# Latents projected inside attention, and attention's loop over batches written out

## The chip, the cores and the metric

The kernel runs on one core of a Trainium2 chip. The metric is the device time of one execution in microseconds, as the median of several runs. The engines of the core work in parallel and meet at semaphores only: TensorE (PE in the profile, with its weight loads as PEld), VectorE (DVE), ScalarE (ACT), GpSimd (POOL), and SyncE (SP), which here issues nearly all DMAs.

## The reference

Everything is float32. `x` is [8, 1024, 256]: 8 batches of 1024 tokens.

```python
x = layernorm(x + attention(x))
x = layernorm(x + expert_choice_moe(x))   # 8 experts, hidden 1024; untouched by the change

def attention(x):                         # 16 heads of 64, causal
    latent = x @ w_kv_down                # [.., 256] @ [256, 128]
    kv = latent @ w_kv_up                 # [.., 128] @ [128, 2048]
    k, v = kv[..., :1024], kv[..., 1024:]
    q = x @ w_q                           # [.., 256] @ [256, 1024]
    att = softmax(mask(q @ k.T * 64 ** -0.5))
    return (att @ v) @ w_out
```

## The kernel before

**Stages.** `latent_stage`, `attention_stage`, `output_stage`, `choose_stage` and `expert_stage` run one after the other, each a block of its own that begins once every engine has left the one ahead. Only the first two are touched.

**latent_stage** (from line 37). For each batch, 4 float32 matmuls of 128x512 (two halves of the tokens, two halves of the 256 channels) form the latents in a PSUM tile `a_ps`. ScalarE copies them out (line 94) and stores them to a DRAM tensor `lat_d` (line 96). A loop runs twice over four batches.

**attention_stage** (from line 101). The unit of work is a pair of heads: 8 batches with 8 pairs each, `n` = 0 to 63, `m = n % 8`. A pair has 16 slots `s`, one for each of 8 query tiles and 2 heads. Every engine walks through the slots with its own written order (`slots`), which interleaves three pairs. In slot `s` TensorE does the following:

- the scores of slot `s + 3` (lines 373, 374: the queries split into a high and a low float32r part, against the keys), once ScalarE has finished the exponentials of two slots earlier (`exp_done`);
- the transposes of the probabilities of slot `s` (line 389, `turn`) into `t_ps`, or into `s_ps` in slot 14;
- projections for later pairs into the single bank `j_ps`: queries of pair `n + 2` in slots 12 and 15 (`Q_AT`, lines 421 to 423, six matmuls each), keys of pair `n + 1` in slots 2 and 5 (`K_AT`), values of pair `n + 1` in slots 7 and 9 (`V_AT`, line 444);
- the products with the values, `pv` (line 405), in slots 14, 1 and 4.

VectorE takes the masked maximum of each slot (line 598) and its reciprocal sum (line 603), half of the copies out of `t_ps` (line 662), and the low parts of the queries and keys (lines 611, 614). ScalarE has the exponentials (line 505), the other half of the copies (line 581), the high parts (line 513) and the copies of the values (line 518). GpSimd scales the probabilities (line 247). SyncE stores `y`, loads weights, and places the split queries and keys into `q_hl`, `k_hh` and `k_lz` by DMA, ten issues for each pair.

**Once in a batch, in pair m = 6:** `x_split` makes the parts `b_xt_hi` and `b_xt_lo` of the next batch's x in slots 0, 2, 4 and 6 (lines 534 and 626), and `l_split` the parts `b_lat_hi` and `b_lat_lo` of its latents in slots 14 and 15 (lines 541 and 632). The latents come from `lat_d` by a DMA on SyncE's queue (line 284), which waits until the values of pair 7 are projected.

**The loop.** `over_pairs` (line 184) writes out `first()` and the first half of pair 0, then has a hardware loop of 7 turns on each engine, whose body is 8 whole pairs from the middle of pair 0 to the middle of the next batch's pair 0, and then writes out the last batch. In the loop a wait compares with a register, and instructions that set such registers stand between the others. The loop turns back between slots 7 and 8 of a batch's first pair. `first()` projects the queries, keys and values of pair 0 one after the other through `j_ps`.

Of the kernel before, what the change touches and what calls it, by code (L numbers as in the profile page):

```python
# [36 lines left out]
def latent_stage(nc, x_t, w_down, lat_d):  # L37

    XB = 4
    with ExitStack() as ctx:  # L40
        sb = lambda n, s, d=F32: ctx.enter_context(nc.sbuf_tensor(n, s, d))
        sem = lambda n: ctx.enter_context(nc.semaphore(n))
        wd = sb("wd", [P, KC, RANK])
        xt = [sb(f"a_xt{v}", [P, KC, T]) for v in range(XB)]
        lat = [sb(f"a_lat{u}", [P, T]) for u in range(2)]
        ps = [ctx.enter_context(nc.psum_tensor(f"a_ps{u}", [P, T], F32)) for u in range(2)]
        w_in, lat_done, lat_copied = sem("a_w_in"), sem("a_lat_done"), sem("a_lat_copied")
        x_in = [sem(f"a_x_in{v}") for v in range(XB)]
        lat_out = [sem(f"a_lat_out{u}") for u in range(2)]
        block = ctx.enter_context(nc.Block())  # L50

        @block.sync
        def _(sp):
            def load_x(b, v):
                sp.dma_start(xt[v][:], x_t.rearrange("(k p) (b t) -> p k b t", p=P, t=T)[:, :, bass.ds(b, 1), :]
                             .rearrange("p k o t -> p k (o t)")).then_inc(x_in[v], 16)

            sp.dma_start(wd[:], w_down.rearrange("(k p) r -> p k r", p=P)).then_inc(w_in, 16)
            for v in range(XB):
                load_x(v, v)  # L60
            with sp.Fori(1, B // XB) as i:
                for v in range(XB):
                    b = XB * i + v

                    sp.wait_ge(lat_done, b - XB + 2)
                    load_x(b, v)

        @block.tensor
        def _(pe):

            for signal in (lat_done, lat_copied, *lat_out):
                pe.sem_inc(signal, 1)
            pe.wait_ge(w_in, 16)
            with pe.Fori(0, B // XB) as i:
                for v in range(XB):
                    b = XB * i + v
                    pe.wait_ge(x_in[v], 16 * i + 16)

                    pe.wait_ge(lat_copied, b if v else b + 1)
                    for c in range(T // HALF):  # L80
                        for k in range(KC):
                            mm = pe.matmul(ps[v % 2][:, c * HALF:(c + 1) * HALF], wd[:, k, :],
                                           xt[v][:, k, c * HALF:(c + 1) * HALF], start=(k == 0), stop=(k == KC - 1))
                    mm.then_inc(lat_done, 1)

        @block.scalar
        def _(act):
            with act.Fori(0, B // XB) as i:
                for v in range(XB):
                    b, u = XB * i + v, v % 2  # L90
                    act.wait_ge(lat_done, b + 2)

                    act.wait_ge(lat_out[u], 16 * (XB // 2 * i + v // 2) + 1)
                    act.activation(lat[u][:], ps[u][:], ACT.Copy).then_inc(lat_copied, 1)
                    act.wait_ge(lat_copied, b + 2)
                    act.dma_start(lat_d[bass.ds(b, 1), :, :].rearrange("o p t -> p (o t)"),
                                  lat[u][:]).then_inc(lat_out[u], 16)
            for u in range(2):
                act.wait_ge(lat_out[u], 16 * (B // 2) + 1)


def attention_stage(nc, x_t, w_q, w_k, w_v, lat_d, y_d):
# [9 lines left out]
    with ExitStack() as ctx:  # L112
# [7 lines left out]
        lat = sb("b_lat", [P, T])  # L120

# [32 lines left out]
        const_ready, x_in, lat_in = sem("const_ready"), sem("b_x_in"), sem("b_lat_in")  # L154
# [31 lines left out]
        def over_pairs(eng, first, slots):  # L186

            first()
            slots(0, 0, 0, 2)
            with eng.Fori(0, B - 1) as b:
                for m in range(NPAIR):
                    slots(NPAIR * b + m, m, 1, 2)
                    slots(NPAIR * b + m + 1, (m + 1) % NPAIR, 0, 2)
            for n in range(NPAIRS - NPAIR, NPAIRS):
                after = min(2, NPAIRS - 1 - n)
                if n % NPAIR:
                    slots(n, n % NPAIR, 0, after)  # L200
                slots(n, n % NPAIR, 1, after)
# [3 lines left out]
        L_SPLIT = [(NPAIR - 2, s) for s in (14, 15)]  # L205
# [65 lines left out]
        def _(sp):  # L271
# [11 lines left out]
            def load_latent(b):  # L283
                sp.dma_start(lat[:], lat_d[bass.ds(b, 1), :, :].rearrange("o p t -> p (o t)")).then_inc(lat_in, 16)
# [79 lines left out]
        def _(pe):  # L364
# [87 lines left out]
            def first():  # L452
                pe.wait_ge(const_ready, 8)
                for c in range(2):
                    project_q(0, 0, c)
# [1183 lines left out]
```

## Time and profile before

| | us |
|---|---|
| median of 3 runs (3380.58 to 3381.19) | 3380.62 |
| the profiled execution | 3380.8 |
| its span in the trace | 3379.1 |
| latent stage and the start of attention, up to the first scores | 81.7 |
| attention, from the first scores to its last store of y | 2121.5 |
| the rest (output, choice, experts) | about 1176 |

The table's stages are read from the times at which TensorE's first scores (81.66) and SyncE's last store of `y` (2203.2) start. The span is counted from the first instruction, and 1.7 us lie around it. Positions in the trace are microseconds from the span's start.

### The profile page before, as it was taken

What the parts mean: (1) busy time and instruction counts of PE and PEld (TensorE: products, weight loads), DVE (VectorE), ACT (ScalarE), POOL (GpSimd) and SP (SyncE); (2) the same over time, 40 slices, a digit from 0 to 9 for tenths busy, and PEclk for the clock granted to TensorE, in tenths of its full rate; (3) what the DMA queues carried; (4) which work ended last, traced back from release to release, by engine and by line L of the source; (5) the groups of instructions that cost most, each with busy time, mean ns of one, the idle gap of its engine ahead of it and who ended that gap; (6) DMA issues with size and microseconds to landing.
All of it is one profiled execution on the core that took longest, in us unless ns stands there. A gap on an engine that the chain in (4) does not pass through costs nothing. (4 is left out here: it accounts for less than half of the span.)

```text
span 3379.1 us, 69338 instructions
## 1 busy us (share of the span) xinstructions
PE 3130.4 (93%) x20382; PEld 2506.5 (74%) x20382; DVE 2092.6 (62%) x5849; ACT 1868.3 (55%) x4063; POOL 1371.8 (41%) x1543
## 2 busy tenths in 40 slices
PE   5999999999999999999999999979908999999995
PEld 2777676777677677777677777679907999899995
DVE  1667666667666666666666666656684555555555
ACT  2667676667666676667666666633203433333335
POOL 0334343334344343334333343312214565645555
PEclk7999999999999999999999999989958999999998
DMA  6444444445445444444445444267502333323327
GB/s 209 99 121 117 101 115 108 108 98 126 99 110 121 108 112 112 114 98 119 112 100 121 114 110 98 66 254 267 186 33 65 68 76 70 76 34 68 76 55 209
DMA packets 184389, 376.22 MB, mean 111 GB/s; under 512 B 23872, under 2 KB 108224, under 8 KB 181952
## 3 DMA queue, kind: packets, MB, share of 16 engines
q1 hardware_dynamic: 153152, 316.91, 35.8%
q0 software_dynamic: 29696, 50.48, 7.5%
q8 instruction: 176, 2.88, 0.4%
q10 hardware_dynamic: 1152, 4.19, 0.3%
q14 instruction: 213, 1.74, 0.2%
HBM read 123.97 MB, written 79.76 MB: 60 GB/s over the span
## 5 line engine op out<-in xcount | busy, mean ns | idle before, releaser
L247 POOL TENSOR_SCALAR prob<-prob,inv 128x128 f32<-128x128 f32 (+7 forms) x1024 | 770.4, 752 | 1301.8 <-DVE inv L603 1301.8
L598 DVE CUSTOM_DVE_ANT_0 s_ps<-s_ps,mask 128x128 f32<-128x128 f32 (+7 forms) x1024 | 781.5, 763 | 664.1 <-PE s_ps L374 649.0
L505 ACT ACTIVATE prob<-s_ps,neg_max 128x128 f32<-128x128 f32 (+7 forms) x1024 | 759.5, 742 | 348.5 <-DVE neg_max L598 327.0
L373 PE MATMUL s_ps<-k_hh,q_hl 128*128 128x512 f32 (+3 forms) x1536 | 591.7, 386 | 46.5 <-ACT prob L505 28.5
L389 PE MATMUL t_ps<-ident,prob 128*128 128x128 f32 x4096 | 611.7, 274 | 1.0 <-ACT prob_t L581 0.5
L405 PE MATMUL o_ps<-prob_t,v 128*64 128x512 f32 (+3 forms) x3072 | 537.5, 492 | 1.5 <-DVE y L620 1.5
L581 ACT ACTIVATE prob_t<-t_ps 128x512 f32<-128x512 f32 (+3 forms) x704 | 376.8, 535 | 290.3 <-PE t_ps L389 284.4
L374 PE MATMUL s_ps<-k_lz,q_hl 128*128 128x512 f32 (+3 forms) x1536 | 516.0, 348 | 0.0
L389 PEld LDWEIGHTS t_ps<-ident,prob 128*128 128x128 f32 x4096 | 478.7, 141 | 47.5 <-DVE prob_t L662 1.2
L373 PEld LDWEIGHTS s_ps<-k_hh,q_hl 128*128 128x128 f32 x1536 | 290.6, 189 | 195.8 <-issue 82.3
L405 PEld LDWEIGHTS o_ps<-prob_t,v 128*64 128x64 f32 x3072 | 204.0, 136 | 285.1 <-issue 266.4
L662 DVE COPY prob_t<-t_ps 128x128 f32<-128x128 f32 (+3 forms) x704 | 321.6, 457 | 29.3 <-PE t_ps L389 29.3
L374 PEld LDWEIGHTS s_ps<-k_lz,q_hl 128*128 128x128 f32 x1536 | 292.4, 190 | 32.6
L1424 PE MATMUL e_y<-w_hi,hid_hi 128*128 128x256 f32 (+1 forms) x1088 | 308.0, 283 | 0.0
L1426 PE MATMUL e_y<-w_hi,hid_lo 128*128 128x256 f32 (+1 forms) x1088 | 303.6, 279 | 0.0
L1425 PE MATMUL e_y<-w_lo,hid_hi 128*128 128x256 f32 (+1 forms) x1088 | 303.5, 279 | 0.0
L1473 ACT ACTIVATE raw<-e_h,b1s 128x512 f32<-128x512 f32 (+3 forms) x320 | 186.4, 601 | 139.4 <-PE e_h L1411 105.4
L1528 DVE CAST hid_hi<-raw 128x512 fp32r<-128x512 f32 (+3 forms) x320 | 173.8, 550 | 120.5 <-ACT raw L1473 110.3
L1462 ACT ACTIVATE yg<-yb,gate 128x256 f32<-128x256 f32 x128 | 59.2, 503 | 333.1 <-DVE yb L1552 308.1
L1349 POOL DMA_INDIRECT acc_d<-yg,idx x128 | 210.6, 1645 | 75.1 <-ACT yg L1462 41.2
L1409 PE MATMUL e_h<-tok_hi,w_hi 128*128 128x512 f32 (+3 forms) x640 | 227.3, 355 | 13.5 <-ACT raw L1473 6.8
L1411 PE MATMUL e_h<-tok_hi,w_lo 128*128 128x512 f32 (+3 forms) x640 | 225.5, 352 | 0.0
(157 smaller groups left out, 5547.5 us busy)
## 6 DMA issues: line engine op xcount, KB each, us to landing
k_hh<-k_high SPq DMA_DIRECT2D x256, 256.0 KB, 4.5
q_hl<-q_high SPq DMA_DIRECT2D x128, 256.0 KB, 3.6
q_hl<-q_low SPq DMA_DIRECT2D x128, 256.0 KB, 4.1
k_lz<-k_low SPq DMA_DIRECT2D x128, 256.0 KB, 4.9
y_d<-y SPq DMA_DIRECT2D x128, 256.0 KB, 4.3
c_yt<-y_d SPq DMA_DIRECT2D x16, 2048.0 KB, 8.3
w_raw<-w SPq DMA_DIRECT2D x16, 1024.0 KB
a_xt<-x_t SPq DMA_DIRECT2D x8, 1024.0 KB, 9.5
```

The source lines that it names most:

```text
L247: pool.tensor_scalar(pr, pr, inv[:, s % 4:s % 4 + 1], 1.0, ALU.mult, ALU.mult).then_inc(norm_done, 1)
L373: pe.matmul(out, q_hl[u][h][:, cols], k_hh[u][h][:, w], start=True, stop=False)
L374: mm = pe.matmul(out, q_hl[u][h][:, cols], k_lz[u][h][:, w], start=False, stop=True)
L389: mm = pe.transpose(turned_in(s, k)[:, j * P:(j + 1) * P], prob[s % 4][:, (first + j) * P:(first + j + 1) * P], ident[:])
L405: mm = pe.matmul(o_ps[64 * h:64 * h + 64, off:HALF], v[u][:, k, 64 * h:64 * h + 64], prob_t[g][:, h, k, off:HALF], start=(k == 0), stop=(k ...
L505: act.activation(prob[s % 4][:, 0:(q + 1) * P], s_ps[s % 2][:, 0:(q + 1) * P], ACT.Exp, scale=-1.0, bias=neg_max[:, s % 4:s % 4 + 1], accu ...
L581: act.activation(prob_t[g][:, h, b0:b0 + count, q % 4 * P:(q % 4 + 1) * P], turned_in(s, k)[:, 0:count * P].rearrange("p (j c) -> p j c", ...
L598: dve.tensor_tensor_reduce(part, part, mask[:, T - (q + 1) * P:T], 1.0, -MASKED, ALU.add, ALU.min, neg_max[:, s % 4:s % 4 + 1]).then_inc(m ...
L662: dve.tensor_copy(prob_t[g][:, h, b0:b0 + count, q % 4 * P:(q % 4 + 1) * P], turned_in(s, k)[:, 0:count * P].rearrange("p (j c) -> p j c", ...
L1424: pe.matmul(out, hid_hi[:, m, cols], W.w2_hi[u][:, w], start=(m == 0), stop=False)
L1425: pe.matmul(out, hid_hi[:, m, cols], W.w2_lo[u][:, w], start=False, stop=False)
L1426: mm = pe.matmul(out, hid_lo[:, m, cols], W.w2_hi[u][:, w], start=False, stop=(m == HC - 1))
```

## The change

`latent_stage` and the DRAM tensor `lat_d` go. `attention_stage` takes `w_down` and keeps it in three tiles: `wd`, `wd_hi`, `wd_lo`. A new function `project_l` forms the latents of one half of a batch with six float32r matmuls (high by high, high by low, low by high, for two channel halves) from the parts of x that the query projection already uses. For batch 0 this stands at the head of `first()`. For the next batch it stands in pair m = 6, in slots 10 and 14 (`L_AT`). ScalarE's `l_split`, one slot later, first copies the latents from PSUM to `lat` and then makes `lat_hi`. The queries of pair `n + 2` in that pair wait for these copies, since they use the same bank. In `first()` the second halves of all projections go to `o_ps` in place of `j_ps` (`bank`). `over_pairs` writes out all 64 pairs on TensorE, ScalarE, VectorE and GpSimd. SyncE keeps its loops, without the load of the latents.

```diff
-def latent_stage(nc, x_t, w_down, lat_d):
...
-            slots(0, 0, 0, 2)
-            with eng.Fori(0, B - 1) as b:
-                for m in range(NPAIR):
-                    slots(NPAIR * b + m, m, 1, 2)
-                    slots(NPAIR * b + m + 1, (m + 1) % NPAIR, 0, 2)
-            for n in range(NPAIRS - NPAIR, NPAIRS):
+            for n in range(NPAIRS):
                 after = min(2, NPAIRS - 1 - n)
-                if n % NPAIR:
-                    slots(n, n % NPAIR, 0, after)
-                slots(n, n % NPAIR, 1, after)
+                for g in range(2):
+                    slots(n, n % NPAIR, g, after)
...
-        L_SPLIT = [(NPAIR - 2, s) for s in (14, 15)]
+        L_AT = (10, 14)
...
+        def latents(n, m, s):
+            return L_AT.index(s) if m == NPAIR - 2 and s in L_AT and not last_batch(n) else None
+        def bank(n, c):
+            return o_ps if c and isinstance(n, int) and n == 0 else j_ps
...
-                if reload and m_is(m, NPAIR - 2):
-                    sp.wait_ge(proj_done, 6 * n + 12)
-                    sp.sem_inc(passed, 1)
-                    load_latent(b + 1)
...
+            def project_l(b, c):
+                first = isinstance(b, int) and b == 0
+                if c == 0:
+                    pe.wait_ge(x_low, 4 * b + 4)
+                if first:
+                    pe.wait_ge(wd_low, 1)
+                elif c == 0:
+                    pe.wait_ge(v_copied, 2 * NPAIR * b)
+                else:
+                    pe.wait_ge(low_done, 4 * NPAIR * b + 1)
+                out = bank(b, c)
+                for k in range(KC):
+                    pe.matmul(out[:], wd_hi[:, k, :], xt_hi[:, k, halves(c)], start=(k == 0), stop=False)
+                    pe.matmul(out[:], wd_hi[:, k, :], xt_lo[:, k, halves(c)], start=False, stop=False)
+                    mm = pe.matmul(out[:], wd_lo[:, k, :], xt_hi[:, k, halves(c)], start=False, stop=(k == KC - 1))
+                mm.then_inc(lat_done, 1)
+            def latents_copied(b, c):
+                pe.wait_ge(l_copied, 2 * b + c + 1)
...
+                elif fresh:
+                    latents_copied(n >> 3, c)
...
                     turn(n, s)
+                    if latents(n, m, s) is not None:
+                        project_l((n >> 3) + 1, latents(n, m, s))
...
             def l_split(b, i):
-                act.wait_ge(lat_in, 16 * b + 16)
+                act.wait_ge(lat_done, 2 * b + i + 1)
                 if not (isinstance(b, int) and b == 0):
-                    act.wait_ge(proj_done, 6 * NPAIR * b - 2)
+                    act.wait_ge(proj_done, 6 * NPAIR * b)
+                act.activation(lat[:, halves(i)], bank(b, i)[:], ACT.Copy).then_inc(l_copied, 1)
+                act.wait_ge(l_copied, 2 * b + i + 1)
                 act.activation(lat_hi[:, halves(i)], lat[:, halves(i)], ACT.Copy).then_inc(l_high, 1)
...
-                    if (m, s) in L_SPLIT and not last_batch(n):
-                        l_split((n >> 3) + 1, L_SPLIT.index((m, s)))
+                    if latents(n, m, s - 1) is not None:
+                        l_split((n >> 3) + 1, latents(n, m, s - 1))
```

TensorE at the start of attention, before: six matmuls of the first query half, all halves in `j_ps`.

```order
L421 MATMUL j_ps<-b_xt_hi,wqk_hi 128x512 [waits b_x_low,b_w_low,const_ready]
L422 MATMUL j_ps<-b_xt_lo,wqk_hi 128x512
L423 MATMUL j_ps<-b_xt_hi,wqk_lo 128x512
L421 MATMUL j_ps<-b_xt_hi,wqk_hi 128x512
L422 MATMUL j_ps<-b_xt_lo,wqk_hi 128x512
L423 MATMUL j_ps<-b_xt_hi,wqk_lo 128x512
L421 MATMUL j_ps<-b_xt_hi,wqk_hi 128x512 [waits low_done]
```

The same place now (the first half of the latents, then the head of the second, which has a bank of its own).

```order
L358 MATMUL j_ps<-b_xt_hi,wd_hi 128x512 [waits b_wd_low,b_x_low,const_ready]
L359 MATMUL j_ps<-b_xt_lo,wd_hi 128x512
L360 MATMUL j_ps<-b_xt_hi,wd_lo 128x512
L358 MATMUL j_ps<-b_xt_hi,wd_hi 128x512
L359 MATMUL j_ps<-b_xt_lo,wd_hi 128x512
L360 MATMUL j_ps<-b_xt_hi,wd_lo 128x512
L358 MATMUL o_ps<-b_xt_hi,wd_hi 128x512 [waits b_wd_low]
```

The latents stand ahead of the queries, and a second half no longer waits for VectorE to empty the bank.

TensorE in pair m = 6, slot 10 and the head of slot 11, now (line 323 is the transposes, 307 and 308 the scores).

```order
L323 MATMUL t_ps<-ident,prob 128x128 [waits copied_d]
L323 MATMUL t_ps<-ident,prob 128x128
L358 MATMUL j_ps<-b_xt_hi,wd_hi 128x512 [waits v_copied,b_x_low]
L359 MATMUL j_ps<-b_xt_lo,wd_hi 128x512
L360 MATMUL j_ps<-b_xt_hi,wd_lo 128x512
L358 MATMUL j_ps<-b_xt_hi,wd_hi 128x512
L359 MATMUL j_ps<-b_xt_lo,wd_hi 128x512
L360 MATMUL j_ps<-b_xt_hi,wd_lo 128x512
L307 MATMUL s_ps<-k_hh,q_hl 128x512 [waits exp_done]
```

Before, the scores followed the transposes directly; six matmuls stand between them, and the first waits for the copy of the values. The second six stand in the same way in slot 14, ahead of `pv`.

VectorE in pair m = 6, slots 11 and 12, before (line 598 is the maximum, 662 the copy of the transposed tiles).

```order
L598 ISA s_ps,neg_max<-s_ps,mask 128x1024 [waits scores_done]
L598 ISA neg_max 128x1
L603 RECIPROCAL inv<-total 128x1 [waits exp_done]
L660 REGISTER_ALU
L662 COPY prob_t<-t_ps 128x2x128 [waits pv_done1,turned]
L594 REGISTER_ALU
L598 ISA s_ps,neg_max<-s_ps,mask 128x1024 [waits scores_done]
```

And now (line 574 is the maximum, 640 the copy).

```order
L574 ISA s_ps,neg_max<-s_ps,mask 128x1024 [waits scores_done]
L574 ISA neg_max 128x1
L579 RECIPROCAL inv<-total 128x1 [waits exp_done]
L640 COPY prob_t<-t_ps 128x2x128 [waits pv_done1,turned]
L608 TENSOR_TENSOR b_lat_lo<-b_lat,b_lat_hi 128x512 [waits b_l_high]
L574 ISA s_ps,neg_max<-s_ps,mask 128x1024 [waits scores_done]
```

The low part of the latents, which stood in slot 14, is now ahead of the maximum of the last slot's scores and waits there for ScalarE; the register instructions are gone.

## Rows read from the trace of the kernel before

**Rows 1.** The page's head: busy time, share of the span and instructions of each engine.

```profile
PE 3130.4 (93%) x20382; PEld 2506.5 (74%) x20382; DVE 2092.6 (62%) x5849; ACT 1868.3 (55%) x4063; POOL 1371.8 (41%) x1543
```

**Rows 2.** Busy time of each engine in the middle of attention, with granted clock.

```profile
170.00:2230.00 2060.00, 1993.90 (x12437) 1462.94 (x12436) 1361.20 (x4092) 1376.67 (x3170) 797.15 (x1043) 0.99 0.46 111
```

**Rows 3.** TensorE's waits from 170 to 2200: total us, times, longest.

```profile
PE s_ps L373 <- ACT prob L505: 25.9, 69, 2.5
PE s_ps L373 <- issue: 12.9, 4, 3.4
PE j_ps L444 <- DVE k_low L614: 3.9, 7, 0.6
```

**Rows 4.** The same windows view, from slot 12 to the next pair's slot 12.

```profile
1795.85:1828.38 32.53, 32.22 (x202) 23.67 (x202) 21.62 (x67) 22.01 (x52) 12.91 (x18) 1.00 0.45 106
1860.87:1894.02 33.15, 32.28 (x202) 23.68 (x202) 24.01 (x71) 23.87 (x56) 13.89 (x18) 1.00 0.45 105
2024.61:2057.22 32.61, 32.27 (x202) 23.66 (x202) 21.63 (x67) 22.06 (x52) 12.90 (x18) 1.00 0.45 105
```

**Rows 5.** The same view of the six pairs in which the loop turns back, and their sum.

```profile
335.88:371.79 35.91, 32.48 (x202) 23.77 (x203) 21.64 (x67) 22.06 (x52) 12.89 (x18) 1.00 0.48 116
600.08:637.75 37.67, 34.06 (x202) 25.16 (x203) 21.69 (x67) 22.07 (x52) 12.89 (x18) 0.95 0.45 110
...
sum 220.91, PE 201.25 PEld 148.33 DVE 129.99 ACT 132.56 POOL 77.37; mean PE 33.54 PEld 24.72 DVE 21.66 ACT 22.09 POOL 12.89
```

**Rows 6.** Timeline of the start: start us, us, engine, line, instruction, idle before.

```profile
1.37 22.07 SPq L55 DMA_DIRECT2D a_xt<-x_t  x8
...
6.69 16.34 PE L82 MATMUL a_ps<-a_xt,wd 128*128 128x512 f32 x32 [6.69 <-DMA a_xt<-x_t]
...
47.78 0.37 SPq L281 DMA_DIRECT2D b_xt<-x_t  x1
...
50.32 3.62 POOL L239 MEMSET k_lz<- 128x1024 f32 x4
...
54.36 2.17 ACT L534 ACTIVATE b_xt_hi<-b_xt 128x512 fp32r<-128x512 f32 x4
...
55.01 2.99 DVE L626 TENSOR_TENSOR b_xt_lo<-b_xt,b_xt_hi 128x512 fp32r<-128x512 f32 x4 [55.01 <-ACT b_xt_hi L534]
...
58.70 0.63 PE L422 MATMUL j_ps<-b_xt_lo,wqk_hi 128*128 128x512 f32 x1
...
59.13 0.63 PE L423 MATMUL j_ps<-b_xt_hi,wqk_lo 128*128 128x512 f32 x1
...
66.88 0.47 PE L430 MATMUL j_ps<-b_lat_hi,wqk_hi 128*128 128x512 f32 x1 [1.50 <-DVE q_low L611]
...
81.66 0.44 PE L373 MATMUL s_ps<-k_hh,q_hl 128*128 128x128 f32 x1 [4.63 <-DMA k_lz<-k_low]
```

**Rows 7.** Timeline, TensorE, first turn of the loop: start, us, instruction, idle before.

```profile
364.66 0.49 PE L373 MATMUL s_ps<-k_hh,q_hl 128*128 128x512 f32 x1 [3.13 <-issue]
```

**Rows 8.** Timeline of pair m = 6 of a late batch, slots 10 to 14.

```profile
1891.63 0.59 ACT L518 ACTIVATE v<-j_ps 128x512 f32<-128x512 f32 x1
...
1891.89 0.47 PE L373 MATMUL s_ps<-k_hh,q_hl 128*128 128x512 f32 x1
...
1894.02 0.50 PE L373 MATMUL s_ps<-k_hh,q_hl 128*128 128x512 f32 x1 [0.31 <-ACT prob L505]
...
1895.73 0.48 PE L421 MATMUL j_ps<-b_xt_hi,wqk_hi 128*128 128x512 f32 x1
...
1897.21 0.22 PE L373 MATMUL s_ps<-k_hh,q_hl 128*128 128x128 f32 x1
...
1899.25 0.69 DVE L611 SCALAR_TENSOR_TENSOR q_low<-j_ps,q_high 128x512 fp32r<-128x512 f32 x1 [0.33 <-ACT q_high L513]
1899.33 2.37 PE L405 MATMUL o_ps<-prob_t,v 128*64 128x512 f32 x16
```

**Rows 9.** DMA of instructions in the written-out last batch, 1959 to 2189 (packets, MB).

```profile
q8 instruction: 11, 0.18, 0.3%
```

More of the change, by code:

```diff
@@ L34 @@
 BH = B * NE
-def latent_stage(nc, x_t, w_down, lat_d):
[L39 to L99, printed above, removed]
@@ L102, in attention_stage @@
[L102 removed]
+def attention_stage(nc, x_t, w_down, w_q, w_k, w_v, y_d):
     NPAIRS = B * NPAIR
@@ L415, in project_q @@
                     pe.wait_ge(x_low, 4 * (n >> 3) + 4)
-                    if not (isinstance(n, int) and n == 0):
-                        pe.wait_ge(v_copied, 2 * n)
+                if first:
+                    latents_copied(0, c)
+                elif fresh:
+                    latents_copied(n >> 3, c)
+                elif c == 0:
+                    pe.wait_ge(v_copied, 2 * n)
                 else:
                     pe.wait_ge(low_done, 4 * n + 1)
+                out = bank(n, c)
                 for k in range(KC):
-                    pe.matmul(j_ps[:], wqk_hi[u][:, k, :], xt_hi[:, k, halves(c)], start=(k == 0), stop=False)
-                    pe.matmul(j_ps[:], wqk_hi[u][:, k, :], xt_lo[:, k, halves(c)], start=False, stop=False)
-                    mm = pe.matmul(j_ps[:], wqk_lo[u][:, k, :], xt_hi[:, k, halves(c)], start=False, stop=(k == KC - 1))
+                    pe.matmul(out[:], wqk_hi[u][:, k, :], xt_hi[:, k, halves(c)], start=(k == 0), stop=False)
+                    pe.matmul(out[:], wqk_hi[u][:, k, :], xt_lo[:, k, halves(c)], start=False, stop=False)
+                    mm = pe.matmul(out[:], wqk_lo[u][:, k, :], xt_hi[:, k, halves(c)], start=False, stop=(k == KC - 1))
                 mm.then_inc(proj_done, 1)
@@ L428, in project_k @@
                     pe.wait_ge(l_low, 2 * (n >> 3) + 2)
-                pe.wait_ge(low_done, 4 * n + 2 + c)
-                pe.matmul(j_ps[:], wqk_hi[u][:, KC, :], lat_hi[:, halves(c)], start=True, stop=False)
-                pe.matmul(j_ps[:], wqk_hi[u][:, KC, :], lat_lo[:, halves(c)], start=False, stop=False)
-                pe.matmul(j_ps[:], wqk_lo[u][:, KC, :], lat_hi[:, halves(c)], start=False, stop=True
+                pe.wait_ge(low_done, 4 * n + (1 if isinstance(n, int) and n == 0 else 2) + c)
+                out = bank(n, c)
+                pe.matmul(out[:], wqk_hi[u][:, KC, :], lat_hi[:, halves(c)], start=True, stop=False)
+                pe.matmul(out[:], wqk_hi[u][:, KC, :], lat_lo[:, halves(c)], start=False, stop=False)
+                pe.matmul(out[:], wqk_lo[u][:, KC, :], lat_hi[:, halves(c)], start=False, stop=True
                           ).then_inc(proj_done, 1)
             def project_v(n, u, c):
+                first = isinstance(n, int) and n == 0
                 if c == 0:
                     pe.wait_ge(w_in[u], 48 * (n >> 1) + 48)
-                    pe.wait_ge(lat_in, 16 * (n >> 3) + 16)
+                    pe.wait_ge(l_copied, 2 * (n >> 3) + 2)
+                if first:
+                    pe.wait_ge(low_done, 3 + c)
+                elif c == 0:
                     pe.wait_ge(low_done, 4 * n + 4)
@@ L453, in first @@
                 pe.wait_ge(const_ready, 8)
+                for c in range(2):
+                    project_l(0, c)
                 for c in range(2):
@@ L666, in slots @@
                         x_split((n >> 3) + 1, X_SPLIT.index((m, s)))
-                    if (m, s) in L_SPLIT and not last_batch(n):
-                        l_split((n >> 3) + 1, L_SPLIT.index((m, s)))
+                    if latents(n, m, s - 1) is not None:
+                        l_split((n >> 3) + 1, latents(n, m, s - 1))
                     if s - 1 in Q_AT and after >= 2:
```

36 lines of the change are left out of this document (21 added, 15 removed).

## The prediction

> **What bounds the kernel now.** I read the page's head first: TensorE is busy for 93% of the span [rows 1], so the question is which TensorE time the change removes or adds, and not which engine is relieved. The windows view of attention says the same of the long middle part: 1993.9 us of 2060 busy at a granted clock of 0.99, with VectorE and ScalarE at two thirds [rows 2]. Next come TensorE's waits in that stretch [rows 3]. There are only three that count: a short one on ScalarE's exponentials in every pair, 12.9 us put down to "issue", that is, to nothing that the profile shows, in 4 places, and 0.6 us once in a batch on the low part of a key. To see what a pair costs I cut attention at slot 12. An ordinary pair takes 32.53 us, the pair m = 6 with the splits takes 33.15, a pair of the written-out last batch 32.61 [rows 4]. The six pairs in which the loop turns back take 220.91 us together [rows 5]. The reader should see three things in these rows: attention is a chain of TensorE work with hardly a gap, so every matmul added to it lengthens it by its own duration; the turns of the loop are the one large gap; and the last batch is already the new form of the code, with its price per pair. The start is a separate matter: up to 81.66 us there is no score [rows 6].
>
> **1. The start.** The latent stage runs from 0.9 to 47.8 us, where attention's first DMA is issued; from there the first scores are 33.9 us away [rows 6]. Now x is loaded for attention at once. Its issue should stand where the first load of x stands, at 1.37. The first x of the latent stage was used 5.3 us after its issue (6.69), attention's x by 6.6 us after it (47.78 to 54.36). I take 5.6, so 7.0. From the first high part to the last low part it is 3.64 us (54.36 to 58.00): 10.7. The twelve matmuls of the latents start there on a cold array, 0.43 us apart (58.70 to 59.13): 5.1 us, so 15.8. The twelve query matmuls cost 5.1 us if still cold, and 12 x 0.245 = 2.9 if the clock has come up by then, as it did during the latent stage's first stretch: 18.7 to 20.9. ScalarE's and VectorE's pieces (0.6 and 0.7 us) no longer stand between the halves, since these have two banks, and the copies of the latents pass beside the query matmuls. The first key matmul then follows, and from it to the first scores it was 14.8 us before (66.88 to 81.66), most of it DMA of queries and keys in a row on SyncE's queue. Sum: 33.5 to 35.7, and perhaps 1 less for the keys' second bank. I take 34.0, so **-47.7 us**, with -45 and -50 as ends. Cover that is gone: GpSimd's fills, which ended 6.2 us after the issue of x (47.78 to 53.94), end before x is split, as they did [rows 6]. The weights' load is issued right behind x and is wanted only after the latents.
>
> **2. The turns of the loop.** The six pairs are 220.91 - 6 x 32.53 = 25.7 us longer than ordinary ones [rows 5]. The gap itself is some 3.1 us, with every engine at its own branch at that time, TensorE's put down to "issue" [rows 7]. The second of the pairs shown has a granted clock of 0.95 over its length, and the six hold 201.25 us of busy TensorE against 6 x 32.23 in ordinary ones, 7.9 us more: after such a gap part of the work runs at the lower of the two clocks. The seventh turn, which leaves the loop, costs nothing. In the changed kernel TensorE's first backward branch stands in the output stage, and no engine but SyncE has one in attention: **-25.7 us**. SyncE's own branch falls between its keys and its next weights, where no one waits. The Trainium skill, "Runtime: NRT & Kernel Launch", section "Instruction fetch mechanics", says that a taken branch to a place outside the fetched window has to wait for a DMA of that code. The gap of 3.13 us agrees.
>
> **3. Code without registers.** The last batch is written out already: 32.61 us for each of its pairs against 32.53 [rows 4], without any loop gap. The 0.08 to 0.09 us appear ahead of the values' projection. What causes them I can't tell from the trace. Over 56 pairs that were in the loop: **+5.0 us**, with 0 and +10 as ends. By the same section of the Trainium skill, code is fetched block by block ahead of its use, and the crossing is mostly hidden. If it were wholly free the sum would be 5 us lower; the row of the last batch decides for the 5.
>
> **4. The latents' matmuls.** In the pair m = 6 of batches 0 to 6, twice six matmuls. Six such matmuls of the query projection take 1895.73 to 1897.21, 1.48 us [rows 8]. 14 x 1.48 = **+20.7 us**. Nothing hides them, since TensorE has no idle time there. The latents' matmuls of the old stage don't count again; they went with it.
>
> **5. The waits that come with them.** I follow the pair of rows 8 with the new order, on its own times.
> - Slot 10: TensorE has its transposes done at 1891.89, but the bank is free only when the values' copy ends at 1892.22: 0.4 us of wait.
> - Slot 12: the wait of 0.31 us for an exponential (1894.02) is gone, since TensorE comes 1.9 us later: -0.3.
> - Slots 11 to 13: ScalarE now has two copies of 0.6 us (latents, high part) instead of none, and VectorE the low part (0.7 us) between the maxima of slots 14 and 15. This maximum and the copy of transposed tiles behind it come about 2.5 us later, TensorE about 1.9 later. The transposes of slots 12 and 13 and the scores that need the last exponential then wait 0.2 + 0.5 + 0.35 = about 1.0 us.
> - Slot 14: the second six want the bank from VectorE's low part of the queries. That ended at 1899.94, when TensorE had reached `pv` at 1899.33; the lag stays nearly the same after both slid: 0.6 us less what was already waited, so 0.3.
> - Slot 15: `pv` (2.3 us) stands between the latents and the queries that wait for their copy, so nothing there. The keys of pair 8 come in slot 2 of pair 7, far behind the split.
>
> This adds up to +1.1 to +1.4 us; I take **1.15 x 7 = +8.0 us**. The ends: -0.3 x 7 = -2 if VectorE and ScalarE keep up, and +3 us a batch, +21, if every one of these waits is passed on in full. SyncE loses a wait and a load of 0.5 MB there, which costs and gives nothing. The 0.6 us that pair 6 already waits for a key's low part [rows 3] stays.
>
> **Sum** on the profiled execution, 3380.8 us: -47.7 - 25.7 + 5.0 + 20.7 + 8.0 = -39.7, which gives 3341.1. The profile is within 0.2 us of the median, so I predict 3341 for the median as well.
>
> **The rivals.**
> - *The latents' chain costs more.* In pair 6 VectorE and ScalarE are already the fullest of the batch, 24.0 and 23.9 us of 33.15 [rows 4], and one more wait of a microsecond or two would be passed from the maximum to the exponential to the scores. At +3 us a batch the time is 3341 + 13 = 3354. For it: three engines wait for one another within four slots. Against it: the same pair took the four splits of x at a price of 0.6 us in all.
> - *The latents' waits vanish.* If TensorE's added 3 us of work give the others enough room, step 5 is -2 and the time 3331. For it: the others have 8 us spare in the pair. Against it: the low part stands in front of a maximum in the written order.
> - *The branch time isn't won.* If the six gaps were fetching that has to be done at some point of a batch anyway, writing the code out would spread them: 3367. Against it: the written-out last batch, with 11 packets of instructions on that queue [rows 9], has no gap of this kind in its pairs.
> - *Slower than before: fetching straight code holds TensorE up.* It would stand anywhere in the 56 pairs. Without step 3 the sum is 3336.1; slower by 0.2% begins at 3387.6, so this needs 51.5 / 56 = 0.92 us for each pair, about one gap like that of rows 7 in every third pair. A gap in every pair would give 3336 + 56 x 3.1 = 3510. It decides once fetching for TensorE takes longer than executing. The last batch shows a tenth of the 0.92, so I give it little. The Trainium skill's section named above speaks against it as well.
> - *The change doesn't do what it says.* The order of instructions shows that it does; I leave no chance to this.
>
> **How the numbers follow.** My forecast (3334 to 3348): 0.66. Latents' chain dearer, about 3354: 0.14. Waits vanish, about 3331: 0.11. Branch time not won, 3367, or half of it: 0.05. Slower, 3388 and beyond: 0.02. Something between, 3374 to 3387: 0.02. The range takes in both chain cases, with the ends of the start (3 us either way) and of step 3 (5 us either way) partly on top: 3327 to 3358. It leaves out the last three cases and the far ends of the two before, some 0.15 in all. A measurement of this kernel can tell about 0.2% (7 us) from no change. Faster by more than that: 0.96; within it: 0.02; slower: 0.02.
>
> **What would show it.** In the profile of the changed kernel: the first scores of attention at 32 to 36 us; no row with "issue" of 3 us ahead of a score in slot 8, and a granted clock of 1.00 in all pairs; ordinary pairs of 32.6 us through all batches; the pair m = 6 at 37 us (33.15 + 2.96 + 0.09 + 1.15) and waits on ScalarE, VectorE and the values' copy in slots 10 to 14; TensorE's matmuls from `wd` 84 in number after the first twelve, about 1.5 us for each six. I'm wrong if ordinary pairs take more than 33 us, if pair 6 takes more than 40, or if the first scores start after 40 us.

## The result and the profile after

The changed kernel takes 3335.3 us (median of 4 runs, 3334.5 to 3335.9) against 3380.6 for the kernel before beside it: a ratio of 0.9869, with a 95% interval of 0.9857 to 0.9881. The profiled execution took 3334.5 us, with a span of 3332.8. The forecast was 3341 (3327 to 3358), so the sign, the size and most of the terms held. On the later occasions the kernel before had medians of 3377 to 3384 us, so an absolute time from one occasion can be compared with one from another only to some 4 us. In the traces a stage can be cut out, but each is of one execution: the first scores came at 33.42 us here and at 32.61 in the changed kernel's second trace, and the first pair behind them took 25.36 and 26.84 us, at a granted clock of 0.93 and 0.84.

The start in the trace after (start, us, engine, line, instruction, idle before):

```profile
1.36 0.45 SPq L223 DMA_DIRECT2D b_xt<-x_t  x1
...
6.54 2.19 ACT L505 ACTIVATE b_xt_hi<-b_xt 128x512 fp32r<-128x512 f32 x4 [3.03 <-DMA b_xt<-x_t]
7.20 2.50 DVE L602 TENSOR_TENSOR b_xt_lo<-b_xt,b_xt_hi 128x512 fp32r<-128x512 f32 x4 [3.24 <-ACT b_xt_hi L505]
...
9.80 0.76 PE L358 MATMUL j_ps<-b_xt_hi,wd_hi 128*128 128x512 f32 x1 [9.80 <-DVE b_xt_lo L602]
...
15.06 0.51 PE L382 MATMUL j_ps<-b_xt_hi,wqk_hi 128*128 128x512 f32 x1
...
18.33 0.47 PE L392 MATMUL j_ps<-b_lat_hi,wqk_hi 128*128 128x512 f32 x1 [0.26 <-DVE q_low L587]
...
33.42 0.44 PE L307 MATMUL s_ps<-k_hh,q_hl 128*128 128x128 f32 x1 [10.40 <-DMA k_lz<-k_low]
```

These answer to [rows 6]. The first scores come at 33.42 us where they came at 81.66, 48.2 us earlier. TensorE's last wait there is on the DMA of the keys.

TensorE's waits in attention after, from 50 to 2150, in full down to 1 us in total: us, times, longest (the answer to [rows 3]):

```profile
PE s_ps L307 <- ACT prob L476: 19.8, 67, 0.7
PE j_ps L410 <- DVE k_low L590: 4.5, 7, 0.7
PE j_ps L358 <- DVE q_low L587: 2.6, 7, 0.4
PE j_ps L358 <- ACT v L489: 1.1, 7, 0.2
```

The row with "issue" is gone. Two new rows stand in its place, seven waits each, both on the latents' bank: 0.16 us for the copy of the values in slot 10 and 0.36 us for the low part of the queries in slot 14.

The windows view of three pairs in a row of the trace after: an ordinary one, then the pair m = 6, then m = 7. A row has the stretch, its length, the busy time of TensorE, its weight loads, VectorE, ScalarE and GpSimd, then the granted clock, the DMA share and GB/s. The stretches are cut at the first query matmul of slot 12, so the latents' second half (slot 14) lies in the third.

```profile
1751.36:1783.93 32.57, 32.24 (x205) 23.65 (x204) 21.64 (x67) 22.11 (x53) 12.93 (x18) 1.00 0.46 107
1816.56:1851.03 34.47, 33.66 (x211) 24.76 (x210) 24.06 (x71) 24.81 (x57) 13.42 (x18) 1.00 0.45 107
1851.03:1886.11 35.08, 34.22 (x212) 24.74 (x210) 22.68 (x69) 23.70 (x56) 13.90 (x18) 1.00 0.39 92
```

Before, the last two took 33.15 + 32.54 us. The granted clock is 1.00 throughout, and TensorE is busy for 1943.2 of the 1970 us from 130 to 2100. Ordinary pairs alternate between 32.57 and 32.63 us, as those of the old last batch did at 32.61 [rows 4]. The old pairs in which the loop turned back [rows 5] have no counterpart: the same pair now takes 32.6. The prediction's sign "pair m = 6 at 37 us" was misplaced, since a cut at slot 12 leaves the second half of the latents to the next pair: the two together were to take some 70.0 us and take 69.55.

### The profile page after: what moved, and what is told of

The parts are those of the page before. It is cut to its first block and busy times, and to the rows that moved or that the text cites. A ratio compares the mean times of both kernels' runs of the same rounds, so it can differ in the third digit from the quotient of the medians.

```text
span 3332.8 us, 62849 instructions
## 1 busy us (share of the span) xinstructions
PE 3114.2 (93%) x20414; PEld 2500.8 (75%) x20414; DVE 2093.2 (63%) x5850; ACT 1875.5 (56%) x4071; POOL 1376.6 (41%) x1543
```

## The experiments

In each experiment two stretches of the trace can be compared with the changed kernel's own: from 0 to the first scores (33.4), and from there to the last `pv` of attention (33.42 to 2153.97, 2120.6 us; before 81.66 to 2196.55, 2114.9 us). "Attention" below is the second of these.

### The loop put back

```diff
-            for n in range(NPAIRS):
-                after = min(2, NPAIRS - 1 - n)
-                for g in range(2):
-                    slots(n, n % NPAIR, g, after)
+            slots(0, 0, 0, 2)
+            with eng.Fori(0, B - 1) as b:
...
```

> The changed kernel with one part undone: attention's hardware loop of seven turns stands again on all four compute engines, the latents stay inside attention. My theory: the turns cost 25.7 us (six gaps of about 3.1 us and some work at the lower clock) and the register code gives back 5, so 3335.3 + 25.7 - 5.0 = 3356, with six gaps in slot 8 of a batch's first pair and ordinary pairs of 32.53 us. The rival, that the changed kernel won its time at the start and with the latents and hardly with the loop: within 5 us of 3335.

Measured: 3363.7 us (3361.7 to 3364.8), 0.9956 of the kernel before (0.9942 to 0.9971). Attention takes 28.1 us more than in the changed kernel. Its waits of TensorE:

```profile
PE s_ps L313 <- ACT prob L482: 24.7, 63, 2.7
PE s_ps L313 <- issue: 13.4, 4, 3.4
```

and in the windows view a pair with a turn, an ordinary pair of the loop, and another pair with a turn:

```profile
293.91:331.74 37.83, 34.09 (x205) 25.25 (x204) 21.65 (x67) 22.14 (x53) 12.97 (x18) 0.95 0.43 102
...
1541.72:1574.22 32.50, 32.19 (x205) 23.67 (x204) 21.63 (x67) 22.04 (x53) 12.96 (x18) 1.00 0.54 139
1643.74:1681.24 37.50, 33.76 (x205) 24.99 (x204) 21.70 (x67) 22.11 (x53) 12.98 (x18) 0.95 0.43 102
```

The gaps and the quicker ordinary pairs are both there as my theory has them, and the rival is out. The size is above what I expected, 28.1 us against 20.7, for two reasons. The six pairs with a turn are 29.5 us longer than ordinary ones of 32.50, where they were 25.7 before [rows 5]: in all six the busy time is up by 1.6 to 1.9 us, where two of the six before had hardly any of that. And the pairs m = 1 and m = 2 of each batch are 0.1 and 0.4 us longer than ordinary ones, which they weren't before. That is no cost of the turn, since these two pairs of batch 0 are longer as well, and no turn precedes them. The 0.4 stands ahead of the values, which wait for a key's low part; why it comes later there stays open.

### The loop written out in the kernel before

The loop written out as in the change, with the latent stage kept.

> The kernel before with one part of the change alone: attention's loop written out on the four compute engines, the stage of the latents kept. My theory: 3380.6 - 25.7 + 5.0 = 3360, pairs of 32.61 us through all batches and no gap of 3 us. If the two parts of the change don't simply add (the latents fill gaps that the loop leaves), it differs from 3360 by more than 5 us.

Measured: 3361.3 us (3359.6 to 3364.3), 0.9956 of before (0.994 to 0.9973), whose median was 3377.2 on that chip. Its attention is 2094.5 us long, 20.4 less than in the one trace of the kernel before; the prediction had 25.7 - 5.0 = 20.7. By the medians of the whole kernel it is 15.9 us. Its pairs alternate between 32.59 and 32.63, but for three of 32.9 to 33.0 near the end. So this part of the change stands on its own.

The two parts don't simply add, though. By the traces' attention the latents cost 26.1 us with the loop written out (this kernel against the changed one) and 33.8 with the loop kept (the kernel before against the one with the loop put back). Nearly all of the difference of 7.7 us is in the two items named above: 3.8 in the pairs with a turn and some 3.6 in the pairs m = 1 and m = 2. The first may be scatter from one execution to another, the second is the same in every batch.

### Only TensorE written out, and all but TensorE

```diff
+            if eng is nc.tensor:        # the other kernel: eng is not nc.tensor
+                for n in range(NPAIRS):
...
+                return
+            with eng.Fori(0, B - 1) as b:
...
```

> The changed kernel, with the loop written out on TensorE alone and kept on ScalarE, VectorE and GpSimd. Theory A, a turn costs because TensorE itself waits for its code: 3335 to 3338, no gap on TensorE above 1 us. Theory B, every engine waits about as long at its own branch, and TensorE is then held by ScalarE's exponentials: 3350 to 3356, six gaps of 2 to 3 us released by ScalarE. I think B somewhat likelier, since two of the six gaps before were put down to ScalarE.

> The changed kernel, with the loop kept on TensorE alone and written out on ScalarE, VectorE and GpSimd. Both theories expect six gaps of about 3 us put down to issue, with the lower clock behind some of them: 3335 + 19 to 26 = 3354 to 3361, or up to 5 less if the 0.08 us for each pair belong to TensorE's written-out code, so 3350 to 3361. Ordinary pairs then tell whose code costs the 0.08 us: 32.53 if TensorE's, 32.61 if another's.

Measured: 3366.1 us (3362.5 to 3371.2) with TensorE alone written out, 3357.4 us (3355.8 to 3358.7) with TensorE alone in the loop. Their attention takes 36.1 and 22.4 us more than the changed kernel's; the trace of the first is of its slowest execution. TensorE's waits in the first:

```profile
PE s_ps L320 <- ACT prob L489: 22.9, 68, 0.7
PE t_ps L336 <- ACT prob_t L570: 15.8, 7, 3.5
```

and its timeline at one turn, where ScalarE stands still for nothing that the profile shows and TensorE waits for its copy:

```profile
1136.44 0.60 ACT L570 ACTIVATE prob_t<-t_ps 128x512 f32<-128x512 f32 x1 [3.32 <-issue]
...
1137.18 1.30 PE L336 MATMUL t_ps<-ident,prob 128*128 128x128 f32 x5 [3.42 <-ACT prob_t L570]
```

The second kernel's wait that counts, and at one of its turns the gap and the DMA of instructions within it (packets, MB, share of the 16 DMA engines' time in 584.90 to 588.33):

```profile
PE s_ps L320 <- issue: 19.0, 6, 3.3
...
588.33 0.79 PE L320 MATMUL s_ps<-k_hh,q_hl 128*128 128x512 f32 x1 [3.30 <-issue]
...
q8 instruction: 1, 0.02, 3.2%
```

An ordinary pair in the windows view, of the second kernel and then of the first:

```profile
1773.95:1806.45 32.50, 32.20 (x205) 23.68 (x204) 21.60 (x67) 22.02 (x53) 12.97 (x18) 1.00 0.46 106
```

```profile
1786.20:1818.84 32.64, 32.30 (x206) 23.66 (x204) 21.64 (x67) 22.09 (x53) 12.96 (x18) 1.00 0.46 107
```

Theory B holds, and more strongly than I had it. TensorE waits for itself at its branch in the second kernel (2.9 to 3.3 us), and ScalarE in the first (1.9 to 3.4 us ahead of its copy, up to 1.8 ahead of an exponential). VectorE shows no row with "issue" in the first, but at the turn shown it starts its maximum at 1134.34, 2.8 us after the scores for it had ended (1131.51). For GpSimd the trace shows nothing either way. With TensorE's wait taken away nothing is won: the others' waits reach it one after another, through the exponentials and through ScalarE's copies out of `t_ps`, and the time is no better than with all four in the loop. I take it that in the full loop these waits lie on top of one another. Writing out the other three and not TensorE won 6 us.

What TensorE waits for at its branch can be read from the DMA packets of instructions. There are two queues of them, q8 with packets of 16 KB and q14 with packets of 8 KB. In attention (100 to 2150) q8 moves 119 packets where TensorE is in the loop and 102 to 104 where it is written out; q14 moves 176 where the others are in the loop and 97 or 98 where they are not. So q8 carries TensorE's code. At each of the six turns of the second kernel one q8 packet starts within 0.1 us of the gap's beginning, or 0.8 after it, and the gap ends 1.55 to 1.60 us after that packet does. The length follows: where the packet took 1.36 us the gap was 2.86, where it took 1.78 the gap was 3.30. The gap is a wait for code.

The second kernel also settles whose code has the price of being written out: 32.50 us with TensorE in the loop, 32.60 to 32.64 with TensorE's code written out. Set side by side, such pairs run alike within 0.1 us up to slot 7; there the first matmul of the values falls back by 0.1 us in the written-out code, behind a recorded wait of 0.02 to 0.05 us for the low part of a key, where the loop's code shows none. Why the same wait ends later there stays open.

### A third of the turns

```diff
+            with eng.Fori(0, 3) as j:
+                for c in range(2):
+                    b = 2 * j + (c + 1)
+                    for m in range(NPAIR):
...
```

> The changed kernel with a loop of three turns whose body holds two batches (48 pairs), on all four compute engines: the loop turns back twice instead of six times. If the cost belongs to the turn, 5.5 us each as the kernel with six turns showed, and the register code is 0.1 us quicker for each of its pairs: 3335 + 11 - 5 = 3341. If it belongs to the form of the code or to the place in a batch: 3355 to 3364, as with six turns.

Measured: 3342.0 us (3341.0 to 3343.1), 0.9877 of before (0.986 to 0.9893). There are two long pairs, 37.2 and 37.4 us, and no others but those with the latents. Attention is 4.4 us longer than in the changed kernel; 4.7 + 4.9 for the turns less 4.8 for 48 pairs of register code makes 4.8. The cost belongs to the turn.

### One bank at the start

```diff
         def bank(n, c):
-            return o_ps if c and isinstance(n, int) and n == 0 else j_ps
+            return j_ps
```

with the waits for the bank that this needs.

> The changed kernel with all projections of the start in the one bank j_ps, so that the second half of each waits until ScalarE and VectorE have emptied it. From the first query matmul to the last low key it was 13.9 us before (58.14 to 72.07) and is 6.7 now (15.06 to 21.80), and the latents add two copies of 0.7: first scores at 40 to 43 instead of 33.4, so 3342 to 3345. The rival, that DMA on SyncE's queue sets the first scores anyway: below 3337.

Measured: 3344.5 us (3341.7 to 3346.0), 0.9884 of before (0.9869 for the changed kernel). Two rows of its timeline (the first values, the first scores):

```profile
27.74 2.05 PE L410 MATMUL j_ps<-wv,b_lat 128*128 128x128 f32 x8 [1.50 <-DVE k_low L590]
...
37.24 0.44 PE L307 MATMUL s_ps<-k_hh,q_hl 128*128 128x128 f32 x1 [4.69 <-DMA k_lz<-k_low]
```

The first scores came at 37.24, not at 40 to 43: of 8 us of waits for the bank 3.8 reach the scores. In both kernels the scores wait for the keys to be placed by DMA, which begins at 27.69 here and at 22.86 in the changed kernel. Attention behind them is 1.8 us longer, and the unchanged rest 1.6. Of the 1.8, 1.5 lie in the first pair, at a granted clock of 0.85; the changed kernel's own second trace has the same first pair (26.84 us, 0.84), so I don't count them. The second bank is worth some 4 of the 48 us at the start by the traces; the medians, from different chips, differ by 9. The rest of the 48 is the latent stage itself. That the median fell into my range of 3342 to 3345 has luck in it: of the 7 to 10 us that I had expected at the start only 4 are there.

### The keys one slot earlier

```diff
-    Q_AT, K_AT, V_AT = (12, 15), (2, 5), (7, 9)
+    Q_AT, K_AT, V_AT = (12, 15), (2, 4), (7, 9)
```

> The changed kernel with the second half of the keys projected in slot 4 instead of slot 5 (K_AT 2, 4), so that pv stands between it and the values that wait for VectorE's low part. If the 0.1 us of each pair in written-out code and the 0.65 us in pair m = 6 are waits for that low part: 57 x 0.1 + 7 x 0.65 = 10 us less, 3325. If the 0.1 us is the fetching or decoding of TensorE's code: only 4.5 us less, 3331. If it pushes the scores' chain: 3335 or above.

Measured: 3428.7 us (3424.6 to 3431.3), 1.0128 of before (1.0111 to 1.0145), 93 us more than the changed kernel. Of my three cases only "3335 or above" covers it, and I had nothing like this size in mind. TensorE's waits:

```profile
PE s_ps L307 <- ACT prob L476: 57.4, 127, 0.7
PE j_ps L392 <- DVE k_low L590: 41.9, 62, 0.7
```

and two rows of an ordinary pair in the timeline:

```profile
146.66 0.50 PE L392 MATMUL j_ps<-b_lat_hi,wqk_hi 128*128 128x512 f32 x1 [0.68 <-DVE k_low L590]
152.82 0.49 PE L307 MATMUL s_ps<-k_hh,q_hl 128*128 128x512 f32 x1 [0.60 <-ACT prob L476]
```

I had looked only at who waits behind the keys. In slot 4 the second half of the keys waits 0.68 us for VectorE to empty the bank of the first half, and a later score waits 0.60 us more. An ordinary pair takes 34.1 us, 1.5 more, and attention is 89.6 us longer in all; another 7.4 us of the profiled execution lie in the unchanged rest, and nothing here explains them. The question it was meant for, what the 0.1 us is, it doesn't answer. It shows that the second half of the keys can't have the bank `j_ps` a slot earlier.

### No latents for batches 1 to 7

```diff
         def latents(n, m, s):
-            return L_AT.index(s) if m == NPAIR - 2 and s in L_AT and not last_batch(n) else None
+            return None
```

> The changed kernel without the latents of batches 1 to 7: their 84 matmuls, copies and splits are left out, and all batches take the latents of batch 0. It prices steps 4 and 5 of the prediction together. By the prediction 20.7 + 8.0 = 28.7, so 3306.6; by the two pairs around it in the changed kernel's trace (69.55 against 65.8 us) 7 x 3.75 = 26.3, so 3309; if TensorE had idle time that took the latents in: above 3320.

Measured: 3310.8 us (3310.4 to 3311.5), 0.9784 of before (0.9768 to 0.9801). It leaves out the later batches' latents, matmuls, copies and splits. Its attention is 25.3 us shorter than the changed kernel's. That is the whole price of steps 4 and 5, against 28.7 predicted: TensorE had no idle time that took the latents in.

### Two variants that go further, and the changed kernel beside them

The loop over experts in the last stage, which turns back once, written out:

```diff
-            with eng.Fori(1, NE // 2 - 1) as i:
+            for i in range(1, NE // 2 - 1):
```

> The changed kernel with the loop over experts in the last stage written out as well, which turns back once in the middle of that stage. There TensorE waited 4.3 us (5.4 before) for nothing that the profile shows. If a turn costs there what it costs in attention, the gap and 1 to 2 us of lower clock go: 6 to 7 us less than the changed kernel beside it. If the code of the written-out stage has to be waited for elsewhere: no difference.

The second half of the latents behind `pv` in slot 14:

```diff
-                    if latents(n, m, s) is not None:
-                        project_l((n >> 3) + 1, latents(n, m, s))
+                    if latents(n, m, s) == 0:
+                        project_l((n >> 3) + 1, 0)
...
                         pv(n, u, 0, values_0[s])
+                    if latents(n, m, s) == 1:
+                        project_l((n >> 3) + 1, 1)
```

> The changed kernel with the second half of the latents behind pv in slot 14 and not ahead of it. The wait of 0.36 us for VectorE's low part of the queries goes, but the queries of slot 15 then have only that slot's scores and transposes (1.1 us) between them and the copy they wait for (0.15 + 0.6 us, and ScalarE has an exponential first). Between 2.5 us less and 3 us more than the changed kernel; I expect no measurable difference.

> The changed kernel itself, on the same chip as its two variants: 3331 to 3339, and a spread over its runs of 1 to 3 us. The kernel before spread over 3376 to 3389 in the earlier runs. If the turns of the loop are what differs from run to run, the changed kernel's spread stays well below that of the kernel before beside it.

Measured on one chip: 3335.0 us (3334.4 to 3335.8) for the changed kernel, 3329.3 (3328.9 to 3333.3) with the experts written out, 3330.7 (3328.6 to 3334.9) with the latents behind `pv`; ratios to before of 0.9861 (0.9847 to 0.9875), 0.9847 (0.9835 to 0.986) and 0.9851 (0.9838 to 0.9864). The intervals overlap, so the times alone prove neither; the traces show where each gain lies. The rest of the kernel behind the last `pv` takes 1171.8 us with the experts written out, and 1178.5 in the changed kernel beside it. TensorE's waits in the loop over experts of the first variant:

```profile
PE e_h L1387 <- ACT raw L1451: 5.2, 1, 5.2
PE e_h L1387 <- issue: 1.2, 1, 1.2
```

The 4.3 us of "issue" at the turn (5.4 before) are gone, and this rest is 6.7 us shorter, as expected. Attention, whose code is the same, is not: its ordinary pairs take 32.63 us on the mean where the changed kernel's take 32.60 in both its traces. The pair m = 7 of the second variant:

```profile
1846.56:1880.95 34.39, 33.92 (x211) 24.80 (x210) 22.66 (x69) 23.59 (x56) 13.93 (x18) 1.00 0.40 93
```

It takes 34.4 us instead of 35.1, seven times, 4.6 us of attention in all, where I had expected no measurable difference: the wait of 0.36 is gone, the six matmuls behind it take 1.49 us instead of 1.61, and the queries of slot 15 don't wait for the copy.

On the spread: the changed kernel's eight runs lie within 1.5 us, those of the kernel before within 3375 to 3389 over all chips. The two variants, with no more turns than the changed kernel, spread over 4 and 6 us, so I can't put the spread down to the turns.

Both together:

> The two variants that were quicker than the changed kernel, together: the loop over experts written out (5.7 us less beside it) and the second half of the latents behind pv (4.3 us less). They lie in different stages, so they should add: 3335.0 - 5.7 - 4.3 = 3325. If the experts' gain was scatter of the code fetching, 3329 to 3331.

Measured: 3327.2 us (3325.5 to 3328.0), 0.9843 of before (0.983 to 0.9856). This beats both kernels. It falls 2 us short of the full sum, all of it in attention (2118.7 us against 2116.0 with the latents' edit alone, whose code there is the same). That is not plain scatter: all 43 ordinary pairs have their part in it, 32.64 us on the mean here against 32.60 there, as they did with the experts alone written out (32.63). So writing out the last stage seems to cost some 2 us in attention. Why stays open.

## Why the prediction was right

| step | predicted | measured |
|---|---|---|
| 1. first scores | 34.0, -47.7 | 33.42, -48.2 |
| 2 and 3. turns of the loop, register code | -25.7 + 5.0 = -20.7 | -20.4 (loop written out alone, by the trace); -28.1 (against the loop put back) |
| 4 and 5. latents' matmuls and waits | +20.7 + 8.0 = +28.7 | +25.3 (left out), +26.1 (loop written out in both, by the trace) |
| behind attention | 0 | -3.7 |
| sum on the profiled execution | -39.7 | -46.3 |

Attention as a whole was to grow by 8.0 us and grew by 5.7 (2114.9 to 2120.6). So 3.7 of the 6.6 us by which the sum is off lie in stages that the change doesn't touch, 2.3 in attention and 0.5 at the start.

**Step 1** held nearly term by term; the other traces with two banks have the first scores at 32.6 to 33.7. x was used 5.2 us after its issue (5.6 assumed); the low parts took 3.3 us (6.54 to 9.80, 3.64 assumed); twelve cold matmuls took 5.26 us (9.80 to 15.06, 5.1 assumed), with the clock up right behind them, and from the first key matmul to the first scores it was 15.1 us (14.8 assumed).

**Steps 2 and 3** held together, on the kernel that the prediction took them from. Their rival "the branch time isn't won" is out, by the missing row of "issue" and by both experiments on the loop. The rival of slow straight code is out: the longest ordinary pairs, four of them and the same four in both traces of the changed kernel, take 32.8 to 32.9 us, 0.2 or 0.3 more than the others. The prediction named every engine's branch but took the size from TensorE's row alone. The experiments show that neither TensorE's branch nor the others' could be left: with the one in the loop 22 us come back, with the others 36. That the 25.7 fit so well has some luck in it, since with the latents in attention the same loop costs 28.1 net.

**Step 4** was right: six matmuls take 1.46 us in slot 10 and 1.61 in slot 14, 21.5 us in all against 20.7.

**Step 5** was the term that was mis-sized: 8.0 us predicted, 25.3 to 26.1 less 21.5 of matmuls = 3.8 to 4.6 us measured. Here are the pieces of the two traces that it was about (pair m = 6 of a late batch). Before, the rows that [rows 8] doesn't have:

```profile
1891.32 0.82 PE L389 MATMUL t_ps<-ident,prob 128*128 128x128 f32 x6
...
1893.26 1.23 DVE L598 CUSTOM_DVE_ANT_0 s_ps<-s_ps,mask 128x1024 f32<-128x1024 f32 x1
...
1895.41 1.23 DVE L598 CUSTOM_DVE_ANT_0 s_ps<-s_ps,mask 128x1024 f32<-128x1024 f32 x1 [0.53 <-PE s_ps L374]
...
1898.09 0.31 PE L373 MATMUL s_ps<-k_hh,q_hl 128*128 128x128 f32 x1
```

After:

```profile
1845.34 0.82 PE L323 MATMUL t_ps<-ident,prob 128*128 128x128 f32 x6
...
1846.32 0.47 PE L358 MATMUL j_ps<-b_xt_hi,wd_hi 128*128 128x512 f32 x1 [0.16 <-ACT v L489]
...
1847.78 0.39 PE L307 MATMUL s_ps<-k_hh,q_hl 128*128 128x512 f32 x1
...
1849.05 1.23 DVE L574 CUSTOM_DVE_ANT_0 s_ps<-s_ps,mask 128x1024 f32<-128x1024 f32 x1 [1.85 <-PE s_ps L308]
...
1849.27 0.47 PE L307 MATMUL s_ps<-k_hh,q_hl 128*128 128x512 f32 x1
...
1850.59 0.69 DVE L608 TENSOR_TENSOR b_lat_lo<-b_lat,b_lat_hi 128x512 fp32r<-128x512 f32 x1
...
1851.20 1.22 DVE L574 CUSTOM_DVE_ANT_0 s_ps<-s_ps,mask 128x1024 f32<-128x1024 f32 x1
...
1853.78 0.33 PE L307 MATMUL s_ps<-k_hh,q_hl 128*128 128x128 f32 x1 [0.15 <-ACT prob L476]
...
1855.47 0.50 PE L358 MATMUL j_ps<-b_xt_hi,wd_hi 128*128 128x512 f32 x1 [0.36 <-DVE q_low L587]
...
1857.08 2.37 PE L339 MATMUL o_ps<-prob_t,v 128*64 128x512 f32 x16
```

The idle times in brackets are less than a wait costs. Before, the scores start 0.57 us behind six transposes whose modelled length is 0.82, so work overlaps; behind a wait it doesn't, and some 0.25 us more are lost. So I go by the starts, counted from the transposes of slot 10 in each trace:

| TensorE | later than before by | what was added on the way |
|---|---|---|
| first matmul of the latents, slot 10 | 0.41 | wait for the values' copy: 0.41 (0.4 predicted) |
| scores in slot 11 | 1.87 | six matmuls: 1.46 |
| scores in slot 12 | 1.23 | the old wait for the exponential is gone: -0.64 (-0.3 predicted) |
| scores in slot 14 | 1.67 | wait for the exponential, +0.40, and 0.04 ahead of it (1.0 predicted) |
| second half of the latents, slot 14 | 2.12 | wait for the low part of the queries, with 0.02 ahead of it: 0.45 (0.3 predicted) |
| `pv` in slot 14 | 3.73 | six matmuls: 1.61 |

7 x 3.73 = 26.1 us, as measured. The two items that were wrong are the wait in slot 12, worth twice its recorded idle time, and the chain through VectorE: 0.40 us (some 0.2 more in one batch) in place of 1.0. The prediction let the low part push the maximum behind it back to 2.5 us. But VectorE had stood idle for 0.53 us ahead of that maximum in the kernel before (1895.41), and the low part of 0.69 us fell into this time: both maxima come 1.77 us later (1849.05 and 1851.20), and the transposes of slots 12 and 13 wait for nothing.

**Behind attention** I predicted nothing, and the profiled execution is 3.7 us shorter there (1182.6 to 1178.8). Of this 1.8 us are the wait at the experts' turn and its neighbour (5.42 + 0.69 against 4.32). In nine of the other ten traces this unchanged rest took 1178.1 to 1181.4 us, in the kernel with the keys earlier 1186.2, and the wait at the turn 4.3 to 5.6. Before, with 1182.6, lies above these nine and after near their lower end, and the kernel before with its loop written out, whose other stages are unchanged too, has 1180.4. So I don't count it as an effect of the change. It is why the result came out nearer to 3335 than to 3338. The two kernels with the experts' stage written out are left out of this count.

## What to carry to other kernels

A hardware loop whose body is long costs a gap at each turn on every engine that runs it, here 4.3 to 5.5 us for each turn with the clock's part, and it was won back only with the loop written out on all four engines; TensorE alone gave nothing, the other three alone 6 us. Work added to the engine that bounds a stage costs its own duration. The waits that it causes elsewhere should be reckoned with the idle time that the other engines have at that very place, and counted from start to start, since the idle time in brackets leaves out the lost overlap. Two changes that are each measured alone need not add: here they differ by 7.7 us from the sum. Before moving a step by one slot, ask both who waits behind it and what it waits for itself: one slot earlier cost 93 us.

## What the runs showed of the hardware

- A turn costs 2.9 to 3.4 us of standstill on TensorE, and 1.9 to 3.4 us on ScalarE with TensorE written out. The Trainium skill, "Runtime: NRT & Kernel Launch", section "Instruction fetch mechanics", says that a taken branch to code outside the fetched window waits for a DMA of it, and the trace agrees: with TensorE alone in the loop a packet of 16 KB on the instruction queue q8 starts at each gap, and the gap ends 1.55 to 1.60 us after it. In the output stage, whose loop has a short body (some 210 matmuls), TensorE shows no wait for "issue" at its turns.
- Behind a gap of about 3 us the granted clock of the pair fell to 0.95, that is, 1.6 to 1.9 us more of busy time, in four of six turns before and in all six with the loop put back. The length of the gap alone doesn't decide it: behind gaps of 3.13 us (364.66, before) and 3.30 us (1128.78, TensorE alone in the loop) it stayed at 1.00, behind one of 2.49 (1423.76, before) it fell.
- Written-out code costs TensorE 0.1 us for each pair of some 205 matmuls against the same code in a loop with registers, all of it at one wait. Why stays open.
